# Attention without a loop, with masks and text denominators off TensorE

## The reference, cut to what matters

```python
def trinity_mask(txt_tok, img_tok):
    sit = img_tok // 3                       # 256
    img_img = (i < img_tok) & (j < img_tok) & (i // sit == j // sit)
    txt_img = (i >= img_tok) & (j < img_tok)
    txt_txt = (i >= img_tok) & (j >= img_tok) & (i >= j)
    return img_img | txt_img | txt_txt

scores = jnp.einsum('bhqd,bhkd->bhqk', qh, kh) * scale
scores = jnp.where(mask[None, None], scores, -jnp.inf)
attn = jax.nn.softmax(scores, axis=-1)
out = jnp.einsum('bhqk,bhkd->bhqd', attn, vh)

x = x + xattn(layernorm(x), ctx, ...)
x = x + ffn(layernorm(x), ...)
```

## Time and profile before

| | us |
|---|---|
| Median of 3 runs | 1364.84 (1364.02 to 1371.99) |
| The profiled execution, its own time | 1364.88 |
| Its span, first to last instruction | 1362.8 |
| Mean granted clock of TensorE | 0.924 |
| PE, DVE, ACT, POOL busy | 1178.1, 873.3, 513.4, 501.4 |

### The profile page before, as it was taken

How to read it: one execution, slowest core, us unless ns; L and a number is a source line. 1 busy time by engine, 2 the same in 40 slices (tenths; PEclk the granted TensorE clock), 3 DMA queues, 4 the chain that set the end, 5 groups by cost and what they waited for, 6 DMA issues and landing times. The chain is left out here.

```text
span 1362.8 us, 22233 instructions
## 1 busy us (share of the span) xinstructions
PE 1178.1 (86%) x7371; PEld 749.5 (55%) x7395; DVE 873.3 (64%) x1271; ACT 513.4 (38%) x635; POOL 501.4 (37%) x265
## 2 busy tenths in 40 slices
PE   5999999990799998999899899943999499997976
PEld 5888888880455555555555555522666244443432
DVE  5555665640656665666566566641798678878976
ACT  3222222220035554555455455531211255553433
POOL 2444444435024444444354444412444212100444
PEclk8999999995559999999999999985999699998998
DMA  6877777665916666565555557669499543101366
GB/s 229 264 258 261 251 240 253 196 198 140 216 39 149 147 149 136 128 152 130 127 126 130 129 125 156 149 165 253 142 267 273 145 141 149 60 0 62 118 260 223
DMA packets 134501, 229.49 MB, mean 168 GB/s; under 512 B 29544, under 2 KB 57992, under 8 KB 133193
## 3 DMA queue, kind: packets, MB, share of 16 engines
q1 hardware_dynamic: 134426, 228.42, 61.2%
HBM read 146.05 MB, written 78.02 MB: 164 GB/s over the span
## 5 line engine op out<-in xcount | busy, mean ns | idle before, releaser
L555 POOL TENSOR_TENSOR a_prob_sums<-a_probs 128x2048 f32<-128x2048 f32 x48 | 218.9, 4560 | 328.4 <-ACT a_probs L572 328.4
L572 ACT ACTIVATE a_probs<-a_st 128x1024 f32<-128x1024 f32 (+2 forms) x262 | 227.7, 893 | 148.2 <-PE a_st L688 114.6
L609 DVE TENSOR_REDUCE a_neg_max_parts<-a_work 128x1 f32<-128x512 f32 (+1 forms) x288 | 187.6, 657 | 86.6 <-PE a_work L664 47.0
L609 DVE TENSOR_REDUCE a_neg_max<-a_work 128x2 f32<-128x512 f32 x216 | 145.9, 690 | 120.5 <-PE a_work L659 118.3
L688 PE MATMUL a_st<-a_q_stack,a_k_stack 97*128 97x512 f32 x396 | 134.6, 424 | 12.5 <-issue 10.3
L659 PE MATMUL a_work<-a_k_stack,a_q_stack 96*128 96x256 f32 x432 | 104.2, 334 | 41.0 <-DMA a_v<-v_scratch 39.7
L664 PE MATMUL a_work<-a_k_stack,a_q_stack 96*128 96x512 f32 (+1 forms) x288 | 132.6, 475 | 4.7 <-DVE a_neg_max L609 0.7
L659 PEld LDWEIGHTS a_work<-a_k_stack,a_q_stack 96*128 96x128 f32 x432 | 74.1, 204 | 85.3 <-DMA a_v<-v_scratch 40.2
L1280 POOL TENSOR_TENSOR d_out<-d_out,kept_ffn_x 128x512 f32<-128x512 f32 x32 | 49.4, 1577 | 123.2 <-DVE d_out L1317 123.2
L664 PEld LDWEIGHTS a_work<-a_k_stack,a_q_stack 96*128 96x128 f32 x288 | 56.1, 199 | 66.8 <-DVE a_neg_max L609 31.5
L1209 PE MATMUL g_gate<-g_xqt,kept_w_gate 128*128 128x512 bf16 x337 | 89.8, 384 | 2.3 <-ACT g_xqt L1121 1.6
(11 more groups left out here) (177 smaller groups left out, 2308.8 us busy)
## 6 DMA issues: line engine op xcount, KB each, us to landing
a_k_stack<-k_split SPq DMA_DIRECT2D x57, 512.0 KB, 7.1
a_q_stack<-q_split SPq DMA_DIRECT2D x57, 512.0 KB, 14.2
kept_ffn_x<-x_scratch SPq DMA_DIRECT2D x14, 1024.0 KB, 7.7
a_v<-v_scratch SPq DMA_DIRECT2D x19, 512.0 KB, 16.5
p_c<-in_ctx_dram SPq DMA_DIRECT2D x8, 1024.0 KB, 8.7
p_x<-in_x_dram SPq DMA_DIRECT2D x8, 1024.0 KB, 10.9
v_scratch<-p_v_stage SPq DMA_DIRECT2D x16, 512.0 KB, 9.2
k_split<-p_stage_hi SPq DMA_DIRECT2D x16, 512.0 KB, 4.2
```

Source lines behind the costliest of these rows:

```text
L555: pool.tensor_tensor(PP[(3 * g + part) % 2][:], PR[2 * part % 4][:], PR[(2 * part + 1) % 4][:], ALU.add).then_inc(summed, 1)
L572: act.activation(PR[kt % 4][:, 2 * hp:2 * hp + 2, 0:w], STB[hp][:, :, 0:w], ACT.Exp, scale=SCALE)\
L609: dve.tensor_reduce(out, src, AX.X, ALU.max, negate=True).then_inc(wfree, 1)
```

## The change

`attend` is written without the loop: all 16 groups stand one after the other, and nothing is loaded or reduced for groups that don't exist. Beside that:

- There are three `work` banks and three single `st` banks. ScalarE takes an exponential for each head (128x512) in place of one for two heads. In a slot, pieces are put between the heads' `score_t`.
- The masks leave TensorE. VectorE reduces a masked piece with one instruction that adds the mask (in SBUF, bf16) and takes the maximum, with a read of its accumulator behind it. GpSimd cuts the diagonal of `probs` of the blocks 6 and 7 with `affine_select`.
- The text denominators leave TensorE but for one product: GpSimd folds the text halves of the pair sums into one another (128x4x256, two times) and adds the blocks 6 and 7 (128x4x256 and 128x4x128). TensorE multiplies three image sums and one text sum.
- The maxima are kept positive (the one row of `k_stack` is -1), `combine` is one `tensor_reduce`, and the turning stands in slot 1, behind two heads of `score_t`.
- The shift row goes from SBUF to SBUF in one DMA. SP issues it ahead of the third group's loads at the start. The stacks of group i+4 are loaded as soon as the last `score_t` of group i is done, its values when `values` of group i is done.
- The first 12 `score_t` of group 0 stand among the last 12 pieces of group 1.

```diff
-S_PER_SLOT = (3, 4, 4, 4, 4, 4, 3, 2)
+S_PER_SLOT = (3, 3, 4, 4, 4, 3, 4, 3)
+TURN_SLOT = 1
 AHEAD = 3
+NST, NWK = 3, 3
...
+            for i in range(2):
+                load_stacks(i)
+                load_values(i)
+            shift_rows(0)
+            load_stacks(2)
+            load_values(2)
+            for i in range(NGRP):
+                if i + 1 < NGRP:
+                    shift_rows(i + 1)
...
+                if i + 4 < NGRP:
+                    sp.wait_ge(stfull, HG * NKT * (i + 1))
+                    load_stacks(i + 4)
...
         @blk.gpsimd
...
+            def pair(i, c):
+                u = 3 * i + c
+                pool.wait_ge(edone, HG * (NKT * i + 2 * c + 2))
+                if u >= 2:
+                    pool.wait_ge(iden, u - 1)
+                if c == 1 and i:
+                    pool.wait_ge(tden, i)
+                pool.tensor_tensor(PP[u % 2][:], PR[2 * c % 4][:], PR[(2 * c + 1) % 4][:], ALU.add).then_inc(paired, 1)
+                pool.wait_ge(paired, u + 1)
+                if c:
+                    text = PP[u % 2][:, :, SIT:]
+                    pool.tensor_tensor(text, text, PP[1 - u % 2][:, :, SIT:], ALU.add).then_inc(folded, 1)
+                    pool.wait_ge(folded, FOLDS * i + c)
+
+            def fold(i, kt):
+                w, n = N - kt * P, kt - IMG // P
+                probs, text = PR[kt % 4][:, :, 0:w], PP[(3 * i + 2) % 2][:, :, 512 - w:]
+                pool.wait_ge(edone, HG * (NKT * i + kt + 1))
+                pool.affine_select(out=PR[kt % 4][:, :, 0:P], in_=PR[kt % 4][:, :, 0:P], pattern=[[0, HG], [1, P]],
+                                   base=0, channel_multiplier=-1, compare_op=ALU.is_ge, fill=0.0).then_inc(cutd, 1)
+                pool.wait_ge(cutd, 2 * i + n + 1)
+                pool.tensor_tensor(text, text, probs, ALU.add).then_inc(folded, 1)
+                pool.wait_ge(folded, FOLDS * i + 3 + n)
...
         @blk.scalar
+                if u >= 4:
+                    was_i, was_kt = (u - 4) // NKT, (u - 4) % NKT
+                    act.wait_ge(pvdone, u - 3)
+                    if was_kt < IMG // P:
+                        act.wait_ge(paired, 3 * was_i + was_kt // 2 + 1)
+                    else:
+                        act.wait_ge(folded, FOLDS * was_i + 3 + was_kt - IMG // P)
...
         @blk.vector
+                if m in (4, 6):
+                    dve.tensor_tensor_reduce(out=MS[:, m // 2 - 2, 0:w], in0=src, in1=K.mask[:, 512 - w:], scale=1.0, scalar=2 * MASKED,
+                                             op0=ALU.add, op1=ALU.max, accum_out=out).then_inc(wfree, 1)
...
         @blk.tensor
+            for k in range(NPC):
+                scores(1, k)
+                if k >= NPC - len(first):
+                    score_t(0, *first[k - NPC + len(first)])
+            for i in range(NGRP):
+                for kt in range(NKT):
+                    u = NKT * i + kt + AHEAD
+                    ahead = u < NKT * NGRP
+                    todo = slot_pieces(kt) if i + 2 < NGRP else []
+                    for j in range(HG):
+                        if ahead:
+                            score_t(u // NKT, u % NKT, j)
+                        if j == 1 and kt == TURN_SLOT and i + 1 < NGRP:
+                            turn_maxima(i + 1)
+                        if j and len(todo) > 1:
+                            scores(i + 2, todo.pop(0))
+                    values(i, kt)
+                    if kt in (1, 3, 5):
+                        pe.wait_ge(paired, 3 * i + kt // 2 + 1)
+                        denominators(IB, PP[(3 * i + kt // 2) % 2], slice(0, SIT)).then_inc(iden, 1)
+                    if kt == NKT - 1:
+                        pe.wait_ge(folded, FOLDS * (i + 1))
+                        denominators(TB, PP[(3 * i + 2) % 2], slice(SIT, 512)).then_inc(tden, 1)
+                    for k in todo:
+                        scores(i + 2, k)
```

More of the change, by code:

```diff
@@ L548, in _ @@
-            with pool.Fori(0, BATCH) as b:
-                for g in range(G):
-                    i = 4 * b + g
-                    for part in range(3):
-                        pool.wait_ge(dendone, 3 * i + part + 1)
-                        pool.wait_ge(edone, 2 * (SLOTS * i + 2 * part + 2))
-                        pool.tensor_tensor(PP[(3 * g + part) % 2][:], PR[2 * part % 4][:], PR[(2 * part + 1) % 4][:],
-                                           ALU.add).then_inc(summed, 1)
+                pool.memset(f32(KS[st][QROWS:QROWS + 1, :, :]), -1.0).then_inc(ones, 1)
@@ L648, in _ @@
+            for k in range(NPC):
+                largest(0, k)
+            rows_out(0)
+            for k in range(NPC):
+                largest(1, k)
+            for i in range(NGRP):
+                for kt in range(NKT):
+                    if kt == TURN_SLOT and i + 1 < NGRP:
+                        rows_out(i + 1)
+                    if i + 2 < NGRP:
+                        for k in slot_pieces(kt):
+                            largest(i + 2, k)
         @blk.tensor
         def _(pe):
-            pe.sem_inc(pvdone, 4)
@@ L663, in scores @@
                     k0, k1 = 512 * part, min(512 * (part + 1), (t + 1) * P)
[L664 to L666 removed]
+                    op = pe.matmul(out[:, 0:k1 - k0], queries(t), keys[:, k0:k1], start=True, stop=True)
                 op.then_inc(wfull, 1)
[L669 to L672 removed]
+                n += 1
@@ new lines, in values, with denominators @@
+                op.then_inc(pvdone, 1)
+            def denominators(bank, sums, cols):
+                for j in range(HG):
+                    op = pe.matmul(bank[j * DH:(j + 1) * DH, 256:512], K.ones[:], sums[:, j, cols], start=False, stop=True,
+                                   skip_group_check=True)
+                return op
+            for k in range(NPC):
+                scores(0, k)
+            turn_maxima(0)
+            pe.wait_ge(ones, 4)
+            first = [(kt, j) for kt in range(AHEAD) for j in range(HG)]
```

355 lines of the change are left out of this document (146 added, 209 removed).

## The result

The changed kernel takes 1235.11 us (median of 4 runs, 1234.17 to 1236.83) and the kernel before 1368.03 beside it: ratio 0.903, 95% interval 0.8995 to 0.9065, faster by 9.7%. The prediction was 1267.5 us with a range from 1244: the direction is right, the gain is 32 us larger than forecast. The profiled execution took 1234.68 us, its span is 1233.0, its mean clock 0.927.

A forecast was written before the change was run, and what follows sets the result against it. TensorE was taken as the bound, 30.5 us a group; afterwards TensorE (25.7) and GpSimd (25.3) chained at 26.0. With prologue and loop savings the attention's copy starts 97.4 us earlier: 1364.9 - 97.4 = 1267.5 us; forecast 1250 to 1291, range 1244 to 1310.

The forecast's parts named there:

- TensorE, 25.7: TensorE's work per attention group: 30.5 us less 1.4 maxima, 1.7 denominators and 1.7 masks gives 25.7, range 25.0 to 26.5.
- The third `work` bank can only help: TensorE's group: single `st` banks cost 0 to 0.3 us a slot, against a like amount gained from the third bank.
- Masks: TensorE's group: masks leaving TensorE save 1.7 us, 0.9 on eight `score_t` and 0.8 on eight pieces.
- Denominators: TensorE's group: text denominators shrink from 3.96 us to four products for one bank, 2.28, saving 1.7 us.
- GpSimd, 25.3: GpSimd's work per group: 22.0 us additions, 1.5 for two cuts, 1.8 for nine waits of 0.20; range 24.4 to 26.3.
- The period, 26.0: Steady attention group: TensorE and GpSimd chained, small waits add up, 26.0 us, between 25.3 and 27.5.
- Nobody waited for it, so I count nothing: Shift row's DMA: the direct path saves a hop in DRAM, but no gain is counted.
- The prologue: Before the first slot: three banks give VectorE's pace, 18.4 us for 28 pieces; first slot at 389.2 instead of 400.9.
- 1 (a costlier GpSimd): Attention groups: GpSimd bounds by more than forecast, 27.5 to 30 us a period, 1291 to 1328 us; chance 0.18.
- 2 (TensorE at 25 or below): Attention groups: GpSimd cheaper, TensorE bounds at 25 or below, last two groups shrink too, 1235 to 1250 us; chance 0.10.
- Rival 4: Attention groups: waits for folds halve TensorE's clock, 19 us more per such group, 1420 with eight; 0.04 together with rival 5.
- rival 5: Attention groups: GpSimd locks out VectorE's masked reductions, eight waits of 1.7 us, 35 us a period, 1390; 0.04 with Rival 4.

## Why the prediction was off, by its own steps

The error is 32.8 us: 10.2 up to T_0, 18.1 over 15 periods, 4.6 behind them (the copy starts 1.2 us behind T_15, as forecast with 1.1).

- **What was right.** Both engines end up as bounds of nearly the same length (24.3 and 24.1; 25.7 and 25.3 were forecast), the last two groups don't get shorter, the loop's 12 us go, the price of GpSimd's additions holds to 0.04 us, VectorE isn't locked out, `combine` makes no wait.
- **TensorE, 25.7 against 24.3: the step that failed** is "The third `work` bank can only help" with its 0 to 0.3 us a slot for the single `st` banks "against a like amount": netted to nothing without a row, the third bank is worth 2.17 us a group. Masks went the other way, 0.95 for 1.7. Denominators: 2 x 0.43 for the text halves of two pair sums, and 0.57 + 0.33 for blocks 6 and 7, 1.76 for 1.7 (no run measured block 6; it is the same product as the 0.43, and at that price the sum below is 24.4). With the 1.4 of the maxima that is 30.5 - 1.4 - 1.76 - 0.95 - 2.17 = 24.2; measured 24.3.
- **GpSimd, 25.3 against 24.1**: the gap after each instruction, 0.08 for 0.20 (1.1 us in nine), and the cut, 0.63 for 0.76 (0.3). The 0.20 of the earlier trace rows was a gap in another stage, behind an operation of another kind. This step had to fail too: with GpSimd at 25.3 the period could not have been 24.3, whatever the bank gave TensorE.
- **The period, 26.0**: I added 0.3 us over the longer engine for "small waits". The trace lists one of 0.2 to 0.3 us on GpSimd in each period and none on TensorE. Together 15 x (24.3 - 26.0) = -25.5 us.
- **Not foreseen: the shift row.** "Nobody waited for it, so I count nothing" looked at the row's own path, and not at the two loads of stacks now issued in the 24 us ahead of it. It cost +7.2 us, of which 4.5 are TensorE's wait and the rest the lower clock behind it, so the periods came to -18.1 and not -25.5. It is of the start only, and a slower group does not always escape it: with periods of 24.1 to 25.5 us the row was late by 2.2 to 7.0 us in six other runs, while with 26.48 and more, or with the turning in slot 0 (25.10), it was in time.
- **The prologue, T_0 10.2 us early.** The second group's pieces began 4.3 us early: the first piece was 3.3 us ahead of the sum's 348.3 (before, TensorE's first wait ended with the load of the values, now with that of the queries; the semaphores are separate), and 28 pieces took 17.5 us for 18.4. The next 16 pieces took 9.1 us for 10.5. The last 12 pieces and `score_t` took 8.1 us for 11.6: I priced them at clock 0.50 all the way, and it was 1.00 from 377 on, after 4.5 us in which most of TensorE's steps were 0.43 us long, one behind the other. That makes 9.2 us at the first slot and 8.7 at pair 1 of group 0 (384.0 for 392.7); the remaining 1.5 are GpSimd's chain, 19.4 us for 20.9.
- **Behind the attention, 4.6 us.** No step of mine: this part took 457.2 to 462.4 us in fifteen kernels with the same code there, and the 4.6 us lie within that. The granted clock goes with it. Where `output` ends and `gate_up` begins it stood at 0.50 for 20.5 us in the changed kernel and for 23.9 in the kernel before, with TensorE mostly idle; the nine profiled executions with 20.5 us took 455.5 to 457.8 us behind the last copy, the eight with 23.9 took 458.5 to 461.1. Why it stood longer, and whether it is the cause of all 4.6, stays open. The two stretches, now and before:

```profile
940.14:960.62 20.48, 5.67 (x26) 3.38 (x28) 9.57 (x22) 6.85 (x8) 3.79 (x7) 0.50 0.38 121
1066.87:1090.76 23.89, 8.13 (x32) 4.31 (x34) 11.09 (x26) 7.86 (x10) 5.99 (x10) 0.50 0.48 132
```

- **The rivals.** 1 (a costlier GpSimd) is out by its own rows. 2 (TensorE at 25 or below) has the time right, by luck in part, and half of its mechanism: GpSimd was cheaper, but the last groups did not shrink, and the 10 us of the start are none of its terms. 4: the clock stayed 1.00 with TensorE busy 20.7 of 24.3 us, where no gap is longer than 0.7 us. In the last group, with 15.3 of 23.9 and two gaps of 2.5 us at the values of a cut block, it was 0.95: at full up to 772.9 and at 0.50 behind it. At the end of the one wait of 4.5 us it was at 0.50 for 6.8 us, so the mechanism is there, and cost some 2.7 us once. This agrees with what the Trainium skill says of gaps in "TensorE: Matmul & The Clock Gate", section "HAM oscillation". 5: the masked reduction runs at 690 ns. The price that the Trainium skill gives in "GPSIMD Engine Reference", section "Engine selection", is borne out: two-input operations of 128x2048 take VectorE 2.29 us (line 982, eight of them) and GpSimd 4.59. The trace of before had such rows too (2.28 us, line 959), and I missed them. No run put a fold on VectorE. With GpSimd relieved of one or two folds, which went to TensorE, the kernel gets no faster, as TensorE stands at the same length.
- **Slips in the sums of the rivals.** Rival 4 starts from 1264 where the forecast is 1267.5 (its 1420 fits the latter). For rival 5, 15 periods of 35 us instead of 26 give 1402, not 1390.

The range began at 1244. It had rival 2 at 0.10, though an unpriced third bank and gaps taken from another stage both pointed down; a bound "from both sides" for the bank would have reached 2 us a group below my sum.

## What to carry to other kernels

Where an engine feeds two others by turns, the number of banks between them and the order in which it alternates are terms of their own: here a third bank was worth 2.2 and 3.4 us of 24, and the interleaving 5.7, far above the 0.2 to 0.5 us of a listed wait. Put a small transfer that somebody waits for ahead of the big ones in its queue, and count the burst at the start, not the steady share. A wait of the engine that bounds can cost more than its length, if its clock falls behind it. When two engines come out equally long, moving work from one to the other gives nothing; look for stretches, as the last two groups here, where only one of them is full.

## What the runs showed of the hardware

- A small DMA of 16 KB took 7.4 us to be issued and 16.0 us to land, behind two loads of 3 MB on the same queue; with the second load behind it these were 0.56 and 2.1 us. A store issued right behind 3.5 MB of loads took 7.6 us to be issued. All other rows and stores of 128 KB of the changed kernel took 0.3 to 0.6 us to be issued.
- At the end of a wait of 4.5 us TensorE's clock was granted at 0.50 for 6.8 us and most of its steps were 0.43 us instead of 0.23; with TensorE busy 20.7 of 24.3 us and no gap over 0.7 us it stayed at 1.00.
- GpSimd's wait for its own last instruction costs 0.08 us; its cut of 512 elements 0.63 us, half a two-input addition of that size (1.28).
- VectorE's addition with a maximum in one instruction (690 ns for 128x512) takes as long as the plain maximum, plus 83 ns to read the result, and isn't slowed by a GpSimd that is busy 23.5 of 24.3 us.
- TensorE and GpSimd are chained to each other several times in a period and 0.2 us apart in length. No wait of TensorE is listed, and where GpSimd bounds (24.13 us, and 25.53 with two more cuts) it takes no longer than the sum of its instructions and gaps (24.2 and 25.6).
